# GpSimd's operations over 1024 and 768 elements, made in pieces of 256

## The chip, the cores and the metric

One core of a Trainium2 chip runs the whole program. The metric is the device time of one execution in microseconds; the median of three runs of the kernel before is 1775.95 us (1771.97 to 1776.2). Besides the runs there is one profiled execution, with a trace of every instruction.

Engines are called by their names: TensorE (PE in the rows; PEld is its weight load), VectorE (DVE), ScalarE (ACT), GpSimd (POOL) and SyncE (SP, which only issues DMAs here).

## The reference, cut to what matters

For each of 32 sequences of T = 512 tokens with C = 256 channels, in float32:

```python
x0 = x                                   # [32, 512, 256]
x = _layernorm(x)
# delta block
h = layernorm(x, dn_g, dn_b)
q, k, v = split(h @ gates_w + gates_b, 3); lr = h @ lr_w + lr_b
k = k / norm(k)
A = tril(k k^T, -1) + I
u = solve_triangular(A, v, lower=True)
y = (q k^T) @ (lr * u)
x = x + y @ out_w + out_b
# MLP
x = x + relu(layernorm(x, mn_g, mn_b) @ w1 + b1) @ w2 + b2
x = x0 + x
# gated FFN with int weights scaled by 1/127, hidden size 768
z = _layernorm(x)
out = x + (silu(z @ wg^T) * (z @ wu^T)) @ wd^T
```

## The kernel before, in words

A sequence is held as 128 partitions by TB = 4 blocks of C = 256 channels, so a whole sequence in SBUF is 1024 elements a partition. Products in full precision are made with split operands: a tile is rounded to its high part (names ending in `_hi`), the low part is the rest (`_lo`), and three matmuls are summed. Each low part is one subtraction of the high part from the whole.

There are two stages. The first one makes, for all sequences, the normalised keys (`kx`), the Gram matrices of the keys (`gg`, 4 diagonal blocks of 128 columns and, behind column OFF = 512, six blocks below the diagonal, 768 columns) and small inverses, and stores them in DRAM. The change does not touch it. The main stage is a loop over 34 rounds, pipelined by hand. In round i the attention part works on sequence i, the MLP and the gate and up products on sequence i-1, and the down product on sequence i-2. Round 0 has no MLP part, rounds 32 and 33 have no attention part.

The order on each engine is written out by hand, in one function per engine that is called once a round (`pe_body`, `dve_body`, `act_body`, `pool_body`); engines wait for each other by semaphores. Each engine takes its instructions in order, so a wait holds up all that stands behind it. What matters around the change, in the order of a round:

- VectorE makes `a0`, the sequence with the attention's result, and its statistics. GpSimd's `pool_norm` (lines 1437 to 1443, four instructions over 4 elements) turns them into scale and shift, and GpSimd and ScalarE normalise two blocks each into `xn` (lines 1450 and 1152).
- VectorE casts the 768 columns of `gg` to `gl_hi` (line 1321), and GpSimd makes `gl_lo` (line 1455).
- GpSimd adds `a0` to `xa`, giving `xa2` (line 1461; both read as xa in the rows), then makes the next `xa` from the input `xt` and the bias `b2_bc` (line 1466, read as 4 blocks with one bias row of 256). The second waits until the first is complete.
- GpSimd makes the normalised input `xh` in four instructions of 256 elements (line 1472). Behind the last one VectorE casts it to `xhm_hi` (line 1347), and GpSimd makes `xhm_lo` (line 1476).
- Between these VectorE makes `wt[3]` (line 1331), the high and low parts of the MLP's hidden layer, `h_hi(0)`, then `x128` (line 1218), `h_lo(0)`, `h_hi(1)`, `z_lo(3)`, `h_lo(1)` (lines 1281 and 1270), and behind the cast `xhm_hi` the combination `wt[2]` (line 1223).
- On TensorE `pe_zstep(3)` (line 938) needs `wt[3]` and `x128`; `pe_zstep(2)`, later in the round, needs `wt[2]`, which stands behind `xhm_hi` on VectorE. `pe_wstep(2)` needs `gl_lo`; `pe_bt(3)` needs `xhm_lo`; the transposes of `xh` (line 921) need `xhm_done`.
- GpSimd has another `pool_norm`, and then `hl`, four subtractions over 512 elements (line 1487).

SyncE reloads `gg` for the next round when `gl_lo` is done, and `xt` when `xb_done` (line 1467) is signalled.

Of the kernel before, what the change touches and what calls it, by code (L numbers as in the profile page):

```python
# [27 lines left out]
ALU = mybir.AluOpType  # L28
ACT = mybir.ActivationFunctionType
F32 = mybir.dt.float32  # L30
# [3 lines left out]
P = 128  # L34
# [7 lines left out]
def wait(eng, sem, value):  # L42

    if isinstance(value, int) and value <= 0:
        return
    eng.wait_ge(sem, value)


def delta_block_kernel(nc, x, dn_g, dn_b, gates_w, gates_b, lr_w, lr_b, out_w, out_b, mn_g, mn_b,
                       w1, b1, w2, b2, w_gate, w_up, w_down, out):  # L50
    NS, T, C = x.shape
    H = w_gate.shape[0]
    TB, CB, HB = T // P, C // P, H // P
    OFF = TB * P
    ROW = {3: OFF, 2: OFF + 3 * P, 1: OFF + 5 * P}
    GCOL = {(i, j): ROW[i] + j * P for i in ROW for j in range(i)}
    GW = OFF + 6 * P
# [25 lines left out]
    with ExitStack() as ctx:  # L83
        def sb(name, shape, dt=F32, c=ctx):
            return c.enter_context(nc.sbuf_tensor(name, shape, dt))
# [3 lines left out]
        def sem(name):  # L89
            held.append(nc.alloc_semaphore(name=name))  # L90
            return held[-1]
# [21 lines left out]
        def pair(name, shape, c=ctx):  # L113

            return sb(name + "_hi", shape, F32R, c=c), sb(name + "_lo", shape, F32R, c=c)
# [6 lines left out]
        b2_bc = sb("b2_bc", [P, C])  # L122
# [5 lines left out]
        xt = sb("xt", [P, TB, C])  # L128
        xh = sb("xh", [P, TB, C])
        xhT2 = pair("xhT", [P, CB, T])  # L130
        kx = sb("kx", [P, KXW])
        gg = sb("gg", [P, GW])
# [69 lines left out]
        with ExitStack() as pre:  # L202
# [293 lines left out]
            def pool_body(pool, i, par, first, left):  # L496
                if left == 2:
                    norms(pool, i + 2, par, 0)
                pool.wait_ge(sq_done, i + 1)
                wait(pool, kn_done, i)  # L500
                pool.tensor_tensor(rn[:, :], ssq[:, :], mhalf4[:, :], ALU.pow).then_inc(rn_done, 1)
                if left == 2:
                    norms(pool, i + 2, par, 1)
                prep_pool(pool, i - PREP)
                if i == INV_FIRST:
                    invert_start(pool, lanes0, 0)
                for q in range(INV_EACH * (i - INV_FIRST), INV_EACH * (i - INV_FIRST + 1)):
                    if 0 <= q < INV_STEPS:
                        invert_step(pool, lanes0, 0, q // 2, q % 2)
                    elif q == INV_STEPS:  # L510
                        invert_flip(pool, lanes0, 0, flipped0)

            def keys_pool(pool):
                for n in range(2):
                    norms(pool, n, n, 0)
                    norms(pool, n, n, 1)
                piped(pool_body, lambda e: None)(pool)
# [304 lines left out]
        with ExitStack() as mc:  # L822
            def mb(name, shape, dt=F32):
                return sb(name, shape, dt, c=mc)
# [6 lines left out]
            xhm2 = pair("xhm", [P, TB, C], c=mc)  # L831
            gl2 = pair("gl", [P, GW - OFF], c=mc)
# [5 lines left out]
            a0 = mb("a0", [P, TB, C])  # L838
# [6 lines left out]
            xa = mb("xa", [P, TB, C])  # L845
            xa2 = mb("xa2", [P, TB, C])
# [26 lines left out]
            xhm_hi, xhm_lo, gl_hi, gl_lo = sem("xhm_hi"), sem("xhm_lo"), sem("gl_hi"), sem("gl_lo")  # L873
# [4 lines left out]
            xb_done, xa_done, sh_done = sem("xb_done"), sem("xa_done"), sem("sh_done")  # L878
# [17 lines left out]
            def after(eng, sem, n, each=1):  # L896

                wait(eng, sem, min(n, NS) * each)
# [17 lines left out]
            with nc.Block() as block:  # L916
# [515 lines left out]
                def pool_norm(pool, n_done, read, n_read, mv_, ls, sc, steps, mvd, done):  # L1432

                    for k in range(CB):
                        after(pool, read[k], n_read)
                    pool.wait_ge(mvd, n_done)
                    pool.tensor_tensor(ls[:, 0, :], mv_[:, :, 1], eps4[:, :], ALU.add).then_inc(steps[0], 1)  # L1437
                    pool.tensor_tensor(ls[:, 1, :], zero4[:, :], mv_[:, :, 0], ALU.subtract).then_inc(steps[1], 1)
                    pool.wait_ge(steps[0], n_done)
                    pool.tensor_tensor(sc[:, 0, :], ls[:, 0, :], mhalf4[:, :], ALU.pow).then_inc(steps[2], 1)  # L1440
                    pool.wait_ge(steps[1], n_done)
                    pool.wait_ge(steps[2], n_done)
                    pool.tensor_tensor(sc[:, 1, :], sc[:, 0, :], ls[:, 1, :], ALU.mult).then_inc(done, 1)  # L1443

                def pool_body(pool, i, att, mlp, down, m, r):
                    if mlp:
                        pool_norm(pool, i, t3_ps, i - 1, mv2, ls2, sc2, l2, mv2_done, ln2_done)
                        pool.wait_ge(ln2_done, i)
                        for j in range(2):
                            op = pool.tensor_scalar(xn[:, j, :], a0[:, j, :], sc2[:, 0, j:j + 1], sc2[:, 1, j:j + 1],  # L1450
                                                    ALU.mult, ALU.add)
                        op.then_inc(xh2_done, 1)
                    if att:
                        pool.wait_ge(gl_hi, i + 1)
                        pool.tensor_tensor(gl2[1][:, :], gg[:, OFF:GW], gl2[0][:, :].bitcast(F32),  # L1455
                                           ALU.subtract).then_inc(gl_lo, 1)
                    if mlp:
                        for j in range(TB):
                            after(pool, x2_ev[j], i - 1)
                        pool.wait_ge(xb_done, i)  # L1460
                        pool.tensor_tensor(xa2[:, :, :], xa[:, :, :], a0[:, :, :], ALU.add).then_inc(xa_done, 1)  # L1461
                    if att:
                        wait(pool, xin, i * 16)
                        pool.wait_ge(kx_in, (i + 1) * 16)
                        after(pool, xa_done, i)
                        pool.tensor_tensor(xa[:, :, :], xt[:, :, :], b2_bc[:, :].unsqueeze(1).broadcast_to([P, TB, C]),  # L1466
                                           ALU.add).then_inc(xb_done, 1)
                        for k in range(CB):
                            after(pool, ht_ps[k], i)
                        after(pool, xhm_lo, i)  # L1470
                        for j in range(TB):
                            op = pool.tensor_scalar(xh[:, j, :], xt[:, j, :], kx[:, E_S + j:E_S + j + 1],  # L1472
                                                    kx[:, E_B + j:E_B + j + 1], ALU.mult, ALU.add)
                        op.then_inc(xhm_done, 1)
                        pool.wait_ge(xhm_hi, i + 1)
                        pool.tensor_tensor(xhm2[1][:, :, :], xh[:, :, :], xhm2[0][:, :, :].bitcast(F32),
                                           ALU.subtract).then_inc(xhm_lo, 1)
                    if mlp:
                        pool_norm(pool, i, t2_ps, i, mv3, ls3, sc3, l3, mv3_done, ln3_done)
                    if att:  # L1480
                        for j in range(TB):
                            after(pool, x2_ev[j], i)
                        pool.tensor_tensor(shf[:, :], kx[:, E_SH:E_SH + TB], zero4[:, :], ALU.add).then_inc(sh_done, 1)
                    for h in range(HB - 2):
                        if mlp:
                            pool.wait_ge(hh_ev[h], i)
                            pool.tensor_tensor(hl[:, h, :], hf[:, h % 2, :], hh[:, h, :].bitcast(F32),  # L1487
                                               ALU.subtract).then_inc(hl_ev[h], 1)

                @block.gpsimd  # L1490
                def _(pool):
                    overlapped(pool_body)(pool)
# [82 lines left out]
```

## Time and profile before

| | |
|---|---|
| median of 3 runs | 1775.95 us |
| profiled execution, its own time | 1777.43 us |
| span of its trace | 1775.1 us |
| mean granted TensorE clock | 0.983 |
| busy: TensorE matmul, VectorE, ScalarE, GpSimd | 1660.2, 1306.2, 774.0, 905.3 us |
| main stage, first and last GpSimd `gl_lo` start | 346.76 us, 1688.21 us |
| a steady round, from one `gl_lo` to the next | 43.30 us |

The profile has views that are used below: the chain of work that ended last, in order of time (what each step waited for, followed back from the end); groups of instructions by line with their mean duration; the instructions of an engine in order of time, with the idle time before each in brackets and what ended it; waits summed by who waited for whom; and stretches of time with the busy time and the granted TensorE clock. Matmuls are pipelined, so their durations overlap. Busy shares alone say little here, since the engines wait for each other within a round.

### The profile page before, as it was taken

What the parts mean: (1) busy time and instruction counts of PE and PEld (TensorE: products, weight loads), DVE (VectorE), ACT (ScalarE), POOL (GpSimd) and SP (SyncE); (2) the same over time, 40 slices, a digit from 0 to 9 for tenths busy, and PEclk for the clock granted to TensorE, in tenths of its full rate; (3) what the DMA queues carried; (4) which work ended last, traced back from release to release, by engine and by line L of the source; (5) the groups of instructions that cost most, each with busy time, mean ns of one, the idle gap of its engine ahead of it and who ended that gap; (6) DMA issues with size and microseconds to landing.
All of it is one profiled execution on the core that took longest, in us unless ns stands there. A gap on an engine that the chain in (4) does not pass through costs nothing.

```text
span 1775.1 us, 31629 instructions
## 1 busy us (share of the span) xinstructions
PE 1660.2 (94%) x11298; PEld 1505.6 (85%) x11298; DVE 1306.2 (74%) x2898; ACT 774.0 (44%) x1658; POOL 905.3 (51%) x1206
## 2 busy tenths in 40 slices
PE   5899999569999999999999999999999999999997
PEld 4899999468888888888888888888888888888886
DVE  4677777247888887788887777888877777777774
ACT  4677777114334333334344434344443333334442
POOL 4456776235555555555555555555555555555551
PEclk8999999789999999999999999999999999999999
DMA  4755565411111121111111211111112111121200
GB/s 114 240 185 192 193 212 191 167 43 43 54 55 55 55 90 54 55 55 55 63 57 55 90 54 55 55 54 55 55 54 78 55 55 55 56 63 61 62 13 24
DMA packets 131698, 145.32 MB, mean 82 GB/s; under 512 B 60885, under 2 KB 113368, under 8 KB 131544
## 3 DMA queue, kind: packets, MB, share of 16 engines
q1 hardware_dynamic: 131544, 143.31, 25.3%
q8 instruction: 91, 1.49, 0.4%
q14 instruction: 63, 0.52, 0.1%
HBM read 82.13 MB, written 61.15 MB: 81 GB/s over the span
## 4 chain that ended last, share of the span: by engine, by line
PE 45%; POOL 19%; issue 8%; DVE 7%; ACT 1%; POOLq 0%; DMA 0%; DVEq 0%; ACTq 0%
PE ps L153 22%; PE ps L1007 13%; POOL xh L1472 6%; POOL xa L1461 4%; POOL xa L1466 4%; PE ps L921 4%; PE ps L938 3%; PE ps L1017 3%; DVE bs L1418 2%; POOL xn L1450 2%; POOL sc L1440 2%; DVE a L1413 2%; DVE wt L1223 1%; POOL sc L1443 1%; PE ps L927 1%
## 5 line engine op out<-in xcount | busy, mean ns | idle before, releaser
L1487 POOL TENSOR_TENSOR hl<-hf,hh 128x512 fp32r<-128x512 f32 x128 | 167.1, 1305 | 406.2 <-ACT hh L1134 406.2
L1017 PE MATMUL ps<-wdT,hh 128*128 128x256 f32 x768 | 204.0, 303 | 0.8 <-ACT sg L1129 0.6
L1017 PE MATMUL ps<-wdT,hl 128*128 128x256 f32 x768 | 187.3, 281 | 2.0 <-DVE hl L1270 2.0
L1265 DVE TENSOR_TENSOR hf<-ps,sg 128x512 f32<-128x512 f32 x192 | 132.4, 690 | 66.2 <-PE ps L1007 63.6
L1134 ACT ACTIVATE hh<-hf 128x512 fp32r<-128x512 f32 x192 | 120.8, 629 | 135.0 <-DVE hf L1265 131.9
L1138 ACT ACTIVATE z_hi<-ps 128x256 fp32r<-128x256 f32 x128 | 49.4, 386 | 288.6 <-PE ps L938 288.6
L1129 ACT ACTIVATE sg<-ps 128x512 f32<-128x512 f32 x192 | 113.9, 593 | 126.4 <-PE ps L1007 126.4
L1007 PE MATMUL ps<-xh3T_hi,wgT 128*128 128x512 f32 x384 | 154.6, 403 | 1.1 <-DVE xh3T_lo L1270 1.1
L1007 PE MATMUL ps<-xh3T_hi,wuT 128*128 128x512 f32 x384 | 152.5, 397 | 0.0
L1007 PE MATMUL ps<-xh3T_lo,wgT 128*128 128x512 f32 x384 | 152.3, 397 | 0.0
L1007 PE MATMUL ps<-xh3T_lo,wuT 128*128 128x512 f32 x384 | 152.2, 396 | 0.0
L1017 PEld LDWEIGHTS ps<-wdT,hl 128*128 128x128 f32 x768 | 144.9, 189 | 4.0 <-DVE hl L1270 2.4
L1017 PEld LDWEIGHTS ps<-wdT,hh 128*128 128x128 f32 x768 | 144.9, 189 | 3.3 <-ACT sg L1129 1.3
L938 PE MATMUL ps<-wt,x 128*128 128x256 f32 x256 | 86.1, 418 | 40.0 <-issue 31.3
L1437 POOL TENSOR_TENSOR ls<-mv,eps 128x4 f32<-128x4 f32 x64 | 12.9, 202 | 196.7 <-DVE mv L1229 196.7
L1166 ACT ACTIVATE hf<-ps,b1f 128x512 f32<-128x512 f32 x64 | 44.1, 688 | 157.6 <-PE ps L153 157.6
L1472 POOL TENSOR_SCALAR xh<-xt,kx 128x256 f32<-128x256 f32 x128 | 111.6, 884 | 0.0
L927 PE MATMUL ps<-x,p 128*128 128x96 f32 (+2 forms) x768 | 102.8, 278 | 4.0 <-DVE p L1213 2.9
L927 PEld LDWEIGHTS ps<-x,p 128*128 128x128 f32 x768 | 99.3, 197 | 8.4 <-DVE p L1213 3.3
L1455 POOL TENSOR_TENSOR gl_lo<-gg,gl_hi 128x768 fp32r<-128x768 f32 x32 | 59.2, 1849 | 83.3 <-DVE gl_hi L1321 83.3
L1007 PEld LDWEIGHTS ps<-xh3T_hi,wgT 128*128 128x128 f32 x384 | 72.7, 189 | 27.1 <-ACT sg L1129 13.0
L1281 DVE CAST h_hi<-hf 128x512 fp32r<-128x512 f32 x64 | 82.2, 1284 | 18.0 <-ACT hf L1166 18.0
(218 smaller groups left out, 5678.5 us busy)
## 6 DMA issues: line engine op xcount, KB each, us to landing
gg_scratch<-gg SPq DMA_DIRECT2D x32, 640.0 KB, 3.4
gg<-gg_scratch SPq DMA_DIRECT2D x32, 640.0 KB, 3.9
kx_scratch<-kx SPq DMA_DIRECT2D x32, 522.0 KB, 2.9
kx<-kx_scratch SPq DMA_DIRECT2D x32, 522.0 KB, 3.7
xk<-in_L_attn_x_dram SPq DMA_DIRECT2D x32, 512.0 KB, 4.2
xt<-in_L_attn_x_dram SPq DMA_DIRECT2D x32, 512.0 KB, 4.8
out_dram<-ot SPq DMA_DIRECT2D x32, 512.0 KB, 2.9
low_scratch<-gg SPq DMA_DIRECT2D x128, 16.0 KB, 1.5
```

Of the source, the lines that this page charges most:

```text
L153: mm = pe.matmul(dst, a[ka], b[kb], start=start, stop=(stop and n == 0), **kw)
L921: mm = pe.transpose(ps[:, banks[k], blk(j)], src[:, j, blk(k)], ident[:, :])
L927: mm = pe.matmul(ps[:, bank, j * w:(j + 1) * w], lhs(j), rhs[:, j, c0:c0 + w], start=True, stop=True)
L938: pe.matmul(ps[:, A1, 0:C], x64[:, j, :], wt[:, j, :], start=True, stop=True).then_inc(z_ps[j], 1)
L1007: mm = pe.matmul(ps[:, bank, :], w[:, k, blk(h)], part[:, k, :], start=(k == 0 and part is x3h), stop=(k == CB - 1 and part is x3l))
L1017: mm = pe.matmul(ps[:, (FG, FU)[j // 2], (j % 2) * C:(j % 2 + 1) * C], part[:, h, blk(j)], wdT[:, h, :], start=(h == 0 and part is hh), st ...
L1129: act.activation(sg[:, h % 2, :], ps[:, FG, :], ACT.Silu, scale=QUANT).then_inc(sg_ev[h], 1)
L1134: act.activation(hh[:, h, :], hf[:, h % 2, :], ACT.Copy).then_inc(hh_ev[h], 1)
L1265: dve.tensor_tensor(hf[:, h % 2, :], ps[:, up_bank(h), :], sg[:, h % 2, :], ALU.mult).then_inc(hf_ev[h], 1)
L1281: dve.tensor_copy(h12[0][:, m, :], h1[:, m, :]).then_inc(h1_hi[m], 1)
L1472: op = pool.tensor_scalar(xh[:, j, :], xt[:, j, :], kx[:, E_S + j:E_S + j + 1], kx[:, E_B + j:E_B + j + 1], ALU.mult, ALU.add)
L1487: pool.tensor_tensor(hl[:, h, :], hf[:, h % 2, :], hh[:, h, :].bitcast(F32), ALU.subtract).then_inc(hl_ev[h], 1)
```

## The change

Four instructions of `pool_body` are written as loops over blocks of 256 elements. The semaphore is signalled by the last piece, and the waits stand ahead of the first one. The data and the order around them are the same, and the other engines' streams are unchanged.

```diff
-                        pool.tensor_tensor(gl2[1][:, :], gg[:, OFF:GW], gl2[0][:, :].bitcast(F32),
-                                           ALU.subtract).then_inc(gl_lo, 1)
+                        for c in range(0, GW - OFF, 2 * P):
+                            op = pool.tensor_tensor(gl2[1][:, c:c + 2 * P], gg[:, OFF + c:OFF + c + 2 * P],
+                                                    gl2[0][:, c:c + 2 * P].bitcast(F32), ALU.subtract)
+                        op.then_inc(gl_lo, 1)
...
-                        pool.tensor_tensor(xa2[:, :, :], xa[:, :, :], a0[:, :, :], ALU.add).then_inc(xa_done, 1)
+                        for j in range(TB):
+                            op = pool.tensor_tensor(xa2[:, j, :], xa[:, j, :], a0[:, j, :], ALU.add)
+                        op.then_inc(xa_done, 1)
...
-                        pool.tensor_tensor(xa[:, :, :], xt[:, :, :], b2_bc[:, :].unsqueeze(1).broadcast_to([P, TB, C]),
-                                           ALU.add).then_inc(xb_done, 1)
+                        for j in range(TB):
+                            op = pool.tensor_tensor(xa[:, j, :], xt[:, j, :], b2_bc[:, :], ALU.add)
+                        op.then_inc(xb_done, 1)
...
-                        pool.tensor_tensor(xhm2[1][:, :, :], xh[:, :, :], xhm2[0][:, :, :].bitcast(F32),
-                                           ALU.subtract).then_inc(xhm_lo, 1)
+                        for j in range(TB):
+                            op = pool.tensor_tensor(xhm2[1][:, j, :], xh[:, j, :], xhm2[0][:, j, :].bitcast(F32),
+                                                    ALU.subtract)
+                        op.then_inc(xhm_lo, 1)
```

GpSimd's stream in a round of the main stage, from its half of `xn` to the norm behind `xhm_lo`, in the kernel before:

```order
L1450 TENSOR_SCALAR xn<-a,sc 128x256 x2
L1455 TENSOR_TENSOR gl_lo<-gg,gl_hi 128x768
L1461 TENSOR_TENSOR xa<-xa,a 128x1024
L1466 TENSOR_TENSOR xa<-xt,b_bc 128x1024
L1472 TENSOR_SCALAR xh<-xt,kx 128x256 x4
L1476 TENSOR_TENSOR xhm_lo<-xh,xhm_hi 128x1024
L1437 TENSOR_TENSOR ls<-mv,eps 128x4
```

The same place in the changed kernel, whose lines from 1455 on are shifted:

```order
L1450 TENSOR_SCALAR xn<-a,sc 128x256 x2
L1456 TENSOR_TENSOR gl_lo<-gg,gl_hi 128x256 x3
L1464 TENSOR_TENSOR xa<-xa,a 128x256 x4
L1471 TENSOR_TENSOR xa<-xt,b_bc 128x256 x4
L1477 TENSOR_SCALAR xh<-xt,kx 128x256 x4
L1482 TENSOR_TENSOR xhm_lo<-xh,xhm_hi 128x256 x4
L1437 TENSOR_TENSOR ls<-mv,eps 128x4
```

Nothing changed its place; four instructions of a round became fifteen, eleven of them between `xn` and `xh` and four behind. On the other engines the streams are the same row for row.

## Rows read from the trace of the kernel before

**Rows 1.** Chain of waits, round 13: start us, us, what.
```profile
908.10 0.09 POOL gl_lo L1455
...
909.91 2.40 POOL xa L1461
...
914.85 3.55 POOL xh L1472 x4
...
918.42 0.07 DVE xhm_hi L1347
...
919.03 0.49 DVE wt L1223
```

**Rows 2.** Groups on GpSimd, 430 to 1700 us: busy us, mean ns | idle before.
```profile
L1487 POOL TENSOR_TENSOR hl<-hf,hh 128x512 fp32r<-128x512 f32 x116 | 151.6, 1307 | 368.7 <-ACT hh L1134 368.7
...
L1461 POOL TENSOR_TENSOR xa<-xa,a 128x1024 f32<-128x1024 f32 x30 | 71.6, 2387 | 0.0
...
L1455 POOL TENSOR_TENSOR gl_lo<-gg,gl_hi 128x768 fp32r<-128x768 f32 x30 | 55.5, 1851 | 54.2 <-DVE gl_hi L1321 54.2
```

**Rows 3.** VectorE in order of time, round 13: start us, us, instruction [idle before].
```profile
911.03 1.42 DVE L1331 TENSOR_SCALAR wt<-kx 128x256 f32<-128x256 f32 x1
912.85 2.28 DVE L1281 CAST h_hi<-hf 128x512 fp32r<-128x512 f32 x1 [0.41 <-ACT hf L1166]
915.05 0.28 DVE L1218 TENSOR_TENSOR x<-ps,x 128x128 f32<-128x128 f32 x1
915.25 0.84 DVE L1270 TENSOR_TENSOR h_lo<-hf,h_hi 128x512 fp32r<-128x512 f32 x1
916.02 0.41 DVE L1281 CAST h_hi<-hf 128x512 fp32r<-128x512 f32 x1
...
916.90 0.68 DVE L1270 TENSOR_TENSOR h_lo<-hf,h_hi 128x512 fp32r<-128x512 f32 x1
```

**Rows 4.** GpSimd: round 13; xh's duration min/median/max in ns; round 0.
```profile
903.34 0.20 POOL L1438 TENSOR_TENSOR ls<-zero,mv 128x4 f32<-128x4 f32 x1
903.49 1.01 POOL L1440 TENSOR_TENSOR sc<-ls,mhalf 128x4 f32<-128x4 f32 x1
...
912.46 2.39 POOL L1466 TENSOR_TENSOR xa<-xt,b_bc 128x1024 f32<-128x1024 f32 x1 [0.17 <-POOL xa L1461]
...
914.83 0.73 POOL L1472 TENSOR_SCALAR xh<-xt,kx 128x256 f32<-128x256 f32 x1
...
L1472 POOL TENSOR_SCALAR xh<-xt,kx x4: 559/906/1237, 914.8 to 917.8; 128x256 f32<-128x256 f32 x4
...
350.87 2.27 POOL L1472 TENSOR_SCALAR xh<-xt,kx 128x256 f32<-128x256 f32 x4
```

**Rows 5.** Waits of TensorE, 430 to 1700 us: us in total, times, longest.
```profile
PE ps L938 <- issue: 30.9, 30, 1.1
PE ps L938 <- DVE wt L1223: 8.1, 30, 0.3
PE ps L153 <- DVE bt_lo L1270: 0.9, 2, 0.5
```

**Rows 6.** xhm_lo on GpSimd, and TensorE's first product with xhm.
```profile
919.20 2.38 POOL L1476 TENSOR_TENSOR xhm_lo<-xh,xhm_hi 128x1024 fp32r<-128x1024 f32 x1 [0.81 <-DVE xhm_hi L1347]
...
923.02 0.36 PE L153 MATMUL ps<-z_hi,xhm_hi 128*128 128x256 f32 x1
```

**Rows 7.** Round 1: the four xh on GpSimd, and xhm_hi on VectorE.
```profile
393.51 2.79 POOL L1472 TENSOR_SCALAR xh<-xt,kx 128x256 f32<-128x256 f32 x4
...
397.74 0.68 DVE L1347 CAST xhm_hi<-xh 128x1024 fp32r<-128x1024 f32 x1
```

**Rows 8.** Stretches with busy us and PEclk (granted clock); transposes at either level.
```profile
375.70:377.90 2.20, 0.06 (x1) 0.00 (x0) 1.82 (x5) 0.63 (x1) 0.00 (x0) 1.00 0.00 0
...
1748.70:1755.30 6.60, 6.01 (x14) 4.79 (x15) 1.73 (x3) 2.90 (x5) 0.80 (x1) 0.50 0.21 78
...
386.95 1.96 PE L921 MATMUL ps<-ident,xn 128*128 128x128 f32 x8 [1.78 <-POOL xn L1450]
...
1747.12 1.09 PE L921 MATMUL ps<-ident,xn 128*128 128x128 f32 x8 [3.76 <-DVE xn L1248]
```

## What was predicted, before the changed kernel ran

> **What bounds the kernel now.** I read the chain of waits first, over one round of the main stage. From 908.10 us to 918.4 us it runs through GpSimd alone: gl_lo, xa (the add of a0), xa (the add of b2), four xh; then VectorE's cast xhm_hi, its wt and TensorE [rows 1]. The second view is GpSimd's durations by line: 1.85 us for 768 elements, 2.39 us for 1024, 1.31 us for 512 [rows 2]. The third is VectorE in the same stretch: a tensor_scalar of 256 elements that takes 1.42 us, a cast of 512 that takes 2.28 us, and the next such cast 0.41 us [rows 3]. The long ones end just behind the end of a GpSimd instruction: the cast at 912.85 + 2.28 = 915.13, with xa over at 912.46 + 2.39 = 914.85 [rows 3, 4]. So the two engines exclude each other for some of their operations. Fourth, TensorE's waits in rounds 2 to 31: 30.9 us in 30 times before a matmul of line 938, named "issue", which is pe_zstep(3), and 8.1 us in 30 times before pe_zstep(2), for wt; there is next to nothing else [rows 5]. That is 1.03 and 0.27 us a round. The first is x128's: its add starts at 915.05, behind the cast of 2.28 us, and ends at 915.33, and the step follows on it [rows 3]. The second is the end of the GpSimd chain.
>
> By the same view TensorE runs without a pause from pe_zstep(2) to the y products that release the next round, and VectorE, ScalarE and GpSimd's small norm lead on to gl_hi. So a round is as long as this loop, and what GpSimd takes between gl_lo and the last xh is in it in full. The 1.03 us before pe_zstep(3) is not: take it away and TensorE only waits longer before pe_zstep(2).
>
> **What the pieces cost by themselves.** From 512 to 1024 elements a tensor_tensor grows from 1.307 to 2.387 us: 2.109 ns an element, with 0.227 us left over, and 768 elements would be 1.847 us (1.851 measured) [rows 2]. A piece of 256 is then 0.767 us long. Instructions of 4 elements start 0.15 us apart though each is 0.20 long [rows 4], so 0.05 us lies under the one before. A piece takes about 0.71 us of the engine where a quarter of the long one takes 0.54: 0.17 us for each extra instruction. On the chain the change adds 2 (gl_lo) + 3 (xa) + 3 (xa) = 8 of them: 8 x 0.17 = 1.36 us, or by whole groups 3 x 0.71 + 0.05 - 1.85 = 0.33 and 2 x (4 x 0.71 + 0.05 - 2.385) = 1.01, together 1.34 us. I take 1.34. Bounds for one extra instruction: below, the slope with nothing fixed, 0; above, the whole left-over, 0.23.
>
> The three extra pieces of xhm_lo are off the chain: before, it starts at 919.20 and takes 2.38 us, and TensorE asks for it at 923.02, with pe_bt(3) [rows 6]; 0.5 us more still fits, and the order gives GpSimd nothing until the next norm. If the cover were gone it would be 0.5 us a round. The change moves no instruction on any other engine.
>
> **What the shared access gives back.** The four xh take 3.55 us in this round and 2.27 us in round 0, where VectorE has no MLP work [rows 1, 4]: 1.28 us is VectorE's doing. The pieces show whose: the first 0.73, the shortest 0.56, the longest 1.24 us, and from their median (0.906, the middle of 0.73 and the third) the third 1.08 [rows 4]. It is the end of h_hi(0), held back until 914.85, then h_lo(0) with h_hi(1) right behind it, and h_lo(1) [rows 3]. With the xa operations in pieces h_hi(0), which asks at 912.85, gets in at the first border, about when the first xa is over in its stretched form (913.2), where GpSimd pauses for 0.17 us anyway [rows 4]: nothing. h_lo(0) reads two tensors of SBUF and holds the access for some 0.52 us (the delay of the third xh piece, 1.08 - 0.56); at a border it runs beside the fixed part and the 0.05 us of overlap, so I take 0.30. h_hi(1) no longer follows on it, since it needs ScalarE's second relu: 0.25. h_lo(1): 0.30. wt, short, at a border: 0. Sum 0.85 in place of 1.28, a gain of 0.43. Bounds: all four fall into pauses (0) or all cost their undisturbed durations, 0.41 + 0.68 + 0.41 + 0.68 = 2.18 us [rows 3].
>
> So the chain grows by 1.34 - 0.43 = 0.9 us a round. Round 0 and round 1 pay nothing: in round 1 the last xh ends at 393.51 + 2.79 = 396.30 and VectorE casts it only at 397.74 [rows 7]. The last xa, in round 32, is alone on GpSimd, without a queue behind it. That leaves 30 rounds: 30 x 0.9 = 27 us. The profiled execution took 1777.4 us, with a span of 1775.1, so 1804; the median of the runs is 1775.95, 1.5 less, so 1803.
>
> On the sharing, the Trainium skill's page "SBUF — State Buffer" (SBUF: two separate sides) says that the pair of ports which VectorE and GpSimd share is an exclusive lock, taken for the whole instruction, for VectorE operations in a two-port mode or with two SBUF inputs. The trace agrees with who excludes whom (2.28 us for the cast), but not with the whole instruction: the third xh piece grew by 0.52 us beside an h_lo of 0.68. By the page the sum would be 1.34 - 1.28 + 2.18 = 2.24 us a round, the second rival's upper end.
>
> **Rivals.** *TensorE's clock falls.* x128 now comes before TensorE wants it, so TensorE is 1.03 us earlier and its pauses join before pe_zstep(2): 1.03 + 0.27 + 0.9 = 2.2 us. Of pauses this long the trace has both outcomes nearby: with 2.17 us at 375.8 the clock stayed at 2.4 GHz; after 3.76 us up to 1747.1 it was at 1.2 GHz from 1748.7 to 1755.3 [rows 8]. In such a stretch of 6.6 us TensorE takes nearly twice as long (1.96 us for eight transposes at 386.95, in such a stretch, against 1.09 at 1747.12) and sets the round: some 3.3 us lost. For it: 2.2 us is longer than any pause of the steady rounds. Against: just one pause a round, with dense work on both sides. If it strikes in 10 of 30 rounds, 33 us more: 1836; in all, 1902.
>
> *The access costs as much as before, or more.* VectorE gets in only behind a whole group of pieces, since GpSimd's next piece is queued and starts before the last has ended. Then the 1.28 us stays, the round grows by 1.34 us, and the time is 1776 + 40 = 1816; with all four operations paid in full it is 2.24 us and 1843. Against it: VectorE does get in between the xh pieces today, which are queued alike.
>
> *Not slower.* VectorE's operations drop into the fixed parts of the pieces and GpSimd gets its whole 1.28 us back, while an extra piece costs only the 0.15 us between the starts of two tiny ones: 8 x 0.15 - 1.28 = -0.08 us a round, 1774. It decides from the point where an extra piece costs no more than a border saves, 0.16 us. Against it: h_lo holds for 0.52 us, and no border is that long.
>
> *The pieces don't appear as such* (nothing on GpSimd's chain grows, because its stream of short instructions overlaps fully): 1776, hardly likely with 0.15 us between starts.
>
> **How the numbers follow.** Forecast 45%; clock 27%; access as dear as before 14%; not slower 11%; no effect 3%. What can be told from no change is 0.3%, 5.3 us. Slower by more: the first three, 0.86; the other two are shared about evenly, 0.07 and 0.07. The forecast's own range, with a round longer by 0.6 to 1.2 us, is 1794 to 1812. For 8 in 10 I go down to 1788 (0.4 us a round) and up to 1845, which takes in a clock that falls in 12 rounds and the dear access.
>
> **What would show it.** GpSimd's pieces at 0.76 us alone, starting 0.71 us apart; the time from gl_lo's first piece to the end of xh at 11.2 us instead of 10.3; the first h_hi near 0.6 us instead of 2.28; no pause before pe_zstep(3) and one of about 2.2 us before pe_zstep(2); rounds of 44.2 us instead of 43.3. I am wrong if the pieces start 0.6 us apart or less, if the last xh is not later, or if the granted clock is at 1.2 GHz in the rounds.

## The result, and the profile after

| | before | after |
|---|---|---|
| median | 1774.16 us (4 runs, 1771.97 to 1776.2) | 1807.9 us (4 runs, 1805.29 to 1811.15) |
| profiled execution, span | 1777.43, 1775.1 us | 1811.15, 1809.3 us |
| mean granted clock | 0.983 | 0.975 |
| a steady round, gl_lo to gl_lo | 43.30 us | 44.16 us, in six rounds some 1.56 us more |
| gl_lo of round 2 to gl_lo of round 31 | 1257.1 us | 1291.3 us |

The ratio is 1.0185, interval 1.016 to 1.0209: slower by about 33 us.

First the chain of waits in round 13 of the changed kernel, in order of time (start us, us, what); it answers to [rows 1].

```profile
921.07 0.09 POOL gl_lo L1456
921.16 0.61 issue
921.77 1.43 POOL gl_lo L1456 x2
923.20 2.81 POOL xa L1464 x4
...
929.61 2.60 POOL xh L1477 x4
932.21 0.02 issue
932.24 0.06 DVE xhm_hi L1347
```

It runs through the same GpSimd operations, now from 921.07 to 932.2: 11.14 us where it was 10.30 (908.10 to 918.40). The four xh are shorter (2.60 us, 3.55 in [rows 1]), everything ahead of them is longer.

VectorE in the same stretch answers to [rows 3].

```profile
924.00 0.73 DVE L1331 TENSOR_SCALAR wt<-kx 128x256 f32<-128x256 f32 x1
925.83 0.45 DVE L1281 CAST h_hi<-hf 128x512 fp32r<-128x512 f32 x1 [1.10 <-ACT hf L1166]
926.20 0.28 DVE L1218 TENSOR_TENSOR x<-ps,x 128x128 f32<-128x128 f32 x1
926.40 1.05 DVE L1270 TENSOR_TENSOR h_lo<-hf,h_hi 128x512 fp32r<-128x512 f32 x1
928.12 0.90 DVE L1281 CAST h_hi<-hf 128x512 fp32r<-128x512 f32 x1 [0.67 <-ACT hf L1166]
928.95 0.41 DVE L1270 TENSOR_TENSOR z_lo<-ps,z_hi 128x256 fp32r<-128x256 f32 x1
929.28 0.88 DVE L1270 TENSOR_TENSOR h_lo<-hf,h_hi 128x512 fp32r<-128x512 f32 x1
```

GpSimd's pieces of the second xa and of xh in this round (duration in ns, min/median/max, then first and last start) answer to xh's row in [rows 4]:

```profile
L1471 POOL TENSOR_TENSOR xa<-xt,b_bc x4: 733/820/1181, 926.2 to 928.7; 128x256 f32<-128x256 f32 x4
...
L1477 POOL TENSOR_SCALAR xh<-xt,kx x4: 554/557/989, 929.6 to 931.6; 128x256 f32<-128x256 f32 x4
```

One xa piece and one xh piece are far longer than the shortest. By the times it is VectorE's h_lo that had the access there: h_lo(0) and the xa piece of 1.18 us, which starts at 926.86, lie side by side, and so do h_lo(1) and the xh piece of 0.99 us, which starts at 929.60. The first h_hi takes 0.45 us in place of 2.28, wt 0.73 in place of 1.42: VectorE gets in at the borders of GpSimd's pieces. What it gained is not on the path, as TensorE's waits from 430 to 1730 us show (us in total, times, longest), beside [rows 5]:

```profile
PE ps L938 <- DVE wt L1223: 53.2, 29, 1.8
PE ps L153 <- DVE z_lo L1270: 6.1, 29, 0.2
PE ps L153 <- DVE bt_lo L1270: 0.9, 2, 0.4
```

The pause before `pe_zstep(3)` is gone, and the one before `pe_zstep(2)` went from 0.27 to 1.83 us. Last, the stretches right behind this pause in two rounds (busy us of PE, PEld, DVE, ACT, POOL, then the granted clock, DMA share and GB/s), beside [rows 8]:

```profile
444.80:448.10 3.30, 3.30 (x17) 3.30 (x17) 1.96 (x5) 0.18 (x1) 1.50 (x3) 0.50 0.00 0
1113.80:1117.10 3.30, 3.30 (x17) 3.30 (x17) 2.56 (x8) 0.13 (x1) 0.91 (x2) 0.50 0.00 0
```

TensorE is busy throughout, at 1.2 GHz. There are six such stretches in the main loop's steady rounds, none in the kernel before. The account of the 29 rounds between gl_lo of round 2 and gl_lo of round 31, in the profiled executions: 29 x 0.86 = 24.9 us, and 6 x 1.56 = 9.4 us, together 34.3 us, where 34.2 us were measured.

### The profile page after: what moved, and what is told of

It is laid out like the page before. It is cut to its first block, busy times and chain, and to the rows that moved or that the text cites. A ratio compares the mean times of both kernels' runs of the same rounds, so it can differ in the third digit from the quotient of the medians.

```text
span 1809.3 us, 31981 instructions
## 1 busy us (share of the span) xinstructions
PE 1675.1 (93%) x11298; PEld 1521.8 (84%) x11298; DVE 1259.2 (70%) x2898; ACT 770.8 (43%) x1658; POOL 947.7 (52%) x1558
## 4 chain that ended last, share of the span: by engine, by line
PE 44%; POOL 22%; issue 7%; DVE 6%; ACT 1%; POOLq 0%; DMA 0%; DVEq 0%; ACTq 0%
PE ps L153 21%; PE ps L1007 13%; POOL xa L1471 5%; POOL xa L1464 5%; POOL xh L1477 5%; PE ps L921 4%; PE ps L938 3%; PE ps L1017 3%; POOL gl_lo L1456 3%; DVE bs L1418 2%; POOL xn L1450 2%; POOL sc L1440 2%; DVE a L1413 2%; DVE wt L1223 1%; POOL sc L1443 1%
## 5 line engine op out<-in xcount | busy, mean ns | idle before, releaser
L1456 POOL TENSOR_TENSOR gl_lo<-gg,gl_hi 128x256 fp32r<-128x256 f32 x96 | 68.0, 738 | 83.2 <-DVE gl_hi L1321 83.2
L1471 POOL TENSOR_TENSOR xa<-xt,b_bc 128x256 f32<-128x256 f32 x128 | 108.8, 880 | 5.2 <-POOL xa L1464 5.2
L1482 POOL TENSOR_TENSOR xhm_lo<-xh,xhm_hi 128x256 fp32r<-128x256 f32 x128 | 89.9, 737 | 27.9 <-DVE xhm_hi L1347 27.9
L938 PEld LDWEIGHTS ps<-wt,x 128*128 128x128 f32 x256 | 42.1, 194 | 67.6 <-DVE wt L1223 62.2
```

Source lines behind the costliest of these rows:

```text
L938: pe.matmul(ps[:, A1, 0:C], x64[:, j, :], wt[:, j, :], start=True, stop=True).then_inc(z_ps[j], 1)
L1456: op = pool.tensor_tensor(gl2[1][:, c:c + 2 * P], gg[:, OFF + c:OFF + c + 2 * P], gl2[0][:, c:c + 2 * P].bitcast(F32), ALU.subtract)
L1471: op = pool.tensor_tensor(xa[:, j, :], xt[:, j, :], b2_bc[:, :], ALU.add)
```

## The experiments

All kernels are compared with the kernel before on the same chip; "round" is the time from one gl_lo to the next in the steady rounds of the profiled execution.

**One part at a time.** `e1_gl` is the kernel before with only gl_lo in pieces, `e2_xa` with only the two xa, `e3_lo` with only xhm_lo, each by the change's own edit. `e4_half` has the two xa in two pieces of 512:

```diff
-pool.tensor_tensor(xa2[:, :, :], xa[:, :, :], a0[:, :, :], ALU.add).then_inc(xa_done, 1)
+for j in range(0, TB, 2):
+    op = pool.tensor_tensor(xa2[:, j:j + 2, :], xa[:, j:j + 2, :], a0[:, j:j + 2, :], ALU.add)
+op.then_inc(xa_done, 1)
... the same for the add of b2
```

> Only gl_lo is made in pieces of 256, the rest as before. My theory (each extra instruction costs about 0.14 us of GpSimd, and what GpSimd takes from gl_lo to the last xh is in the round in full): three pieces take 2.09 us in the changed kernel's trace where the whole took 1.81, so the round grows by 0.28 us, 30 rounds by 8.4 us, 1782.6 us. Rival (the changed kernel is slower by the falls of TensorE's clock and by VectorE's waits, not by the pieces themselves): no difference here, 1774 us, since no VectorE operation contends in gl_lo's stretch and the pauses of TensorE hardly change.

Measured: 1784.5 us, ratio 1.0048 (1.0033 to 1.0063), round 43.56 us. The theory holds, and to its size: the round grew by 0.26 us, where 0.28 was expected.

> Only the two xa operations are made in pieces of 256. My theory: six extra instructions at 0.15 us are 0.90 us, of which the shared access gives back 0.28 (VectorE's claims cost GpSimd 1.09 us in place of 1.37): 0.62 us a round, and with a pause of some 1.55 us before pe_zstep(2) the clock stays whole: 1793 us. Rival (the access gives nothing back): 0.90 us a round, 1801 us, the first h_hi still short. Rival (the slowdown is gl_lo's or the clock's): below 1780 us.

Measured: 1806.58 us, ratio 1.0176 (1.0158 to 1.0195), round 44.10 us, eight rounds with a stretch at 1.2 GHz. The round grew by 0.80 us, between the theory (0.62) and its first rival (0.90), and I was wrong on the clock, which I had expected to stay whole. By itself this edit does nearly all of the change. GpSimd's rows of round 13 say why gl_lo's pieces add only 0.06 us on top:

```profile
921.98 2.84 POOL L1462 TENSOR_TENSOR xa<-xa,a 128x256 f32<-128x256 f32 x4
924.99 3.67 POOL L1469 TENSOR_TENSOR xa<-xt,b_bc 128x256 f32<-128x256 f32 x4 [0.17 <-POOL xa L1462]
928.65 2.60 POOL L1475 TENSOR_SCALAR xh<-xt,kx 128x256 f32<-128x256 f32 x4
```

Here h_hi(0) comes at 924.93, just as the second xa wants to begin (924.99), and that one's first piece takes 0.97 us where 0.73 is usual. In the changed kernel it comes into the pause between the two xa. What the shared access takes depends on such meetings.

> Only xhm_lo is made in pieces of 256. My theory: it takes 2.82 us in place of 2.38 and still ends at 922.0 by the times of the kernel before, 1 us ahead of pe_bt(3) at 923.02: rounds of 43.30 us, 1774 us. Rival (it is on the path behind another wait, or GpSimd's norm behind it comes late): 0.44 us a round, 1787 us.

Measured: 1777.19 us (10 runs), ratio 1.0003 (0.9987 to 1.002), round 43.30 us. No effect, as expected.

> The two xa operations are made in two pieces of 512, the rest is whole. My theory: two extra instructions cost 0.30 us a round, VectorE gets in at the borders nearly as well as with four pieces (h_hi(0) about 1.3 us long in place of 2.28), and the claims cost 0.2 to 0.3 us less than before: 0 to 0.1 us a round, 1774 to 1777 us. Rival (the access gives back only with a border at the very moment at which VectorE asks): 0.30 us a round, 1783 us. Rival (the borders are where VectorE's blocked operations pile up and cost more than before): above 1785 us.

Measured: 1783.64 us, ratio 1.0043 (1.0028 to 1.0058), round 43.63 us. The first rival was right: two extra instructions cost their 0.3 us, and the access gave nothing back. h_hi(0) still took 1.40 us, h_lo(0) 1.56.

**The price of a piece without VectorE's claims.** Both kernels, with VectorE's split of the hidden layer reduced:

```diff
-dve.tensor_copy(h12[0][:, m, :], h1[:, m, :]).then_inc(h1_hi[m], 1)
+dve.tensor_copy(h12[0][:, m, 0:8], h1[:, m, 0:8]).then_inc(h1_hi[m], 1)
... the same for h_lo, and both tiles zeroed once ahead of the loop
```

> The kernel before with h_hi and h_lo, VectorE's operations on the MLP's hidden layer, over 8 elements in place of 512 (the rest of the hidden layer's split is left out; the tiles are zeroed once). It takes VectorE's claims on the shared access away. My theory: the four xh take 2.2 to 2.3 us (3.55 before), the time from gl_lo to the end of xh falls from 10.28 to about 9.0 us, and a round is shorter by the 0.27 us that TensorE waits before pe_zstep(2) plus up to 1.0 us, as far as TensorE has no other limit: about 42.0 us. Rival (xh is slow by itself in the main stage, for its scalars or for another engine): the four xh stay at 3.5 us.

> The changed kernel with the same left out as in the run before. My theory: from gl_lo to the end of xh 2.09 + 2.80 + 0.21 + 2.80 + 2.2, about 10.1 us, 1.15 to 1.2 us more than the kernel before without claims; so the pieces alone cost 8 x 0.147 us, and the 0.86 us of the full kernels is this less what the access gives back. Rival (pieces cost by their contention with VectorE only): both kernels take the same time from gl_lo to the end of xh.

Measured, one execution each: 1747.68 and 1768.76 us, rounds of 42.50 and 43.07 us. GpSimd in round 13, whole operations, then pieces:

```profile
894.80 1.85 POOL L1459 TENSOR_TENSOR gl_lo<-gg,gl_hi 128x768 fp32r<-128x768 f32 x1 [1.81 <-DVE gl_hi L1321]
896.61 2.38 POOL L1465 TENSOR_TENSOR xa<-xa,a 128x1024 f32<-128x1024 f32 x1
899.16 2.38 POOL L1470 TENSOR_TENSOR xa<-xt,b_bc 128x1024 f32<-128x1024 f32 x1 [0.17 <-POOL xa L1465]
901.52 2.16 POOL L1476 TENSOR_SCALAR xh<-xt,kx 128x256 f32<-128x256 f32 x4
```

```profile
906.71 2.13 POOL L1460 TENSOR_TENSOR gl_lo<-gg,gl_hi 128x256 fp32r<-128x256 f32 x3 [1.81 <-DVE gl_hi L1321]
908.78 2.84 POOL L1468 TENSOR_TENSOR xa<-xa,a 128x256 f32<-128x256 f32 x4
911.80 2.81 POOL L1475 TENSOR_TENSOR xa<-xt,b_bc 128x256 f32<-128x256 f32 x4 [0.17 <-POOL xa L1468]
914.59 2.16 POOL L1481 TENSOR_SCALAR xh<-xt,kx 128x256 f32<-128x256 f32 x4
```

The four xh fall to 2.16 us in both: the slow xh was VectorE's doing. From gl_lo's start to the end of xh it is 8.88 and 10.04 us, so eight extra instructions cost 1.16 us, 0.145 each, with next to no contention for GpSimd: its longest piece in this stretch is 0.77 us. VectorE's wt and, in `e5_before_noclaim`, its reduced cast still had to wait. Even a cast of eight elements took 1.99 us there, until the whole xa was over (899.16 + 2.38 = 901.54):

```profile
899.58 1.99 DVE L1281 CAST h_hi<-hf 128x8 fp32r<-128x8 f32 x1 [0.43 <-ACT hf L1166]
```

The rounds differ by less (0.57 us), since without pieces another wait, 0.75 us before `pe_zstep(3)`, sets the round.

**The clock.** The changed kernel, with TensorE kept at work in its pause:

```diff
+for q in range(6):
+    pe.matmul(ps[:, A1, 0:C], w22[0][:, 0, blk(0)], w22[0][:, 0, :], start=True, stop=True)
 pe_zstep(pe, i, 2)
```

> The changed kernel with six matmuls of 256 columns ahead of pe_zstep(2), into the bank that it overwrites; they run in the pause. My theory (the clock falls where the pause of 1.83 us meets it badly, and each fall costs 1.56 us): the pause is 1.1 us, no stretch at 1.2 GHz in the rounds, all rounds at 44.16 us (and the two with the flip of the inverse at 44.85), some 8 us less than the profiled execution of the changed kernel, about 1801 us, and less spread between runs. Rival (the falls come from something else, or the long rounds are DMA or VectorE): again rounds of 45.7 us, 1807 us.

Measured: 1797.77 us (1796.82 to 1798.93), ratio 1.0121 (1.0106 to 1.0137). All steady rounds take 44.13 us but two, which take 44.87 (the same two are 0.7 us longer in the kernel before); there is no stretch at 1.2 GHz in them, and the pause is 1.12 us. That is 10 us less than the changed kernel's median for 192 matmuls more. So the falls come from the pause: filled in part, it let the clock fall in none of these rounds. Between the two profiled executions gl_lo of round 2 to gl_lo of round 31 is shorter by 9.9 us (1291.3 against 1281.4), the size of six falls. The four runs say the same: their mean granted clocks are 0.983 to 0.985, the changed kernel's 0.975 to 0.979. Of what the two spans differ by beyond that (14.5 us in all), 3.5 us lie ahead of round 2, so not all of the gain is the pause's.

**A better order.** Since xa's second operation is wanted only a round later, the same work can stand elsewhere. First `e8_xh_first`: the four xh ahead of both xa, whole; `e9b_xh_first_pieces` is the same with the xa in pieces.

```diff
 pool.tensor_tensor(gl2[1]...)              # gl_lo
+for j in range(TB): op = pool.tensor_scalar(xh[:, j, :], ...)   # moved up with its waits
 pool.tensor_tensor(xa2...)                 # xa
 pool.tensor_tensor(xa...)
-for j in range(TB): op = pool.tensor_scalar(xh[:, j, :], ...)
```

> The kernel before with xh made ahead of the two xa operations, nothing in pieces. My theory (the chain from gl_lo to xh sets the round): the chain is 2.2 to 2.6 us in place of 8.5 behind gl_lo, xhm_hi no longer waits for it, the 0.27 us before pe_zstep(2) goes, and TensorE's 1.03 us before pe_zstep(3) becomes the limit that is left, since h_hi(0) now stands behind xa (VectorE asks at 912.85, xa would run from 912.3 to 914.7): between 42.2 and 43.0 us a round, 1740 to 1765 us. Rival (the GpSimd chain only seems to be the bound, the round is set by the total of TensorE's work and pauses elsewhere): 43.3 us and 1774 us.

Measured: 1793.45 us, ratio 1.0102 (1.0082 to 1.0121), rounds of 43.81 and 43.95 us. My theory failed, and so did the rival: it is slower than before. VectorE's rows:

```profile
915.17 1.89 DVE L1281 CAST h_hi<-hf 128x512 fp32r<-128x512 f32 x1 [1.16 <-ACT hf L1166]
916.98 0.28 DVE L1218 TENSOR_TENSOR x<-ps,x 128x128 f32<-128x128 f32 x1
917.18 2.69 DVE L1270 TENSOR_TENSOR h_lo<-hf,h_hi 128x512 fp32r<-128x512 f32 x1
```

The cast waits for the first xa, h_lo for the whole second one; z_lo(3) stands behind them, and TensorE waits 1.15 us for it.

> xh ahead of the two xa operations as in the run before (which was slower: VectorE's h_hi(0) took 1.89 us and its h_lo(0) 2.69 us behind whole xa operations, so z_lo(3) came late and TensorE waited 0.65 and 1.14 us), now with the xa operations in pieces of 256. My theory (whole operations cost VectorE, pieces cost GpSimd; here GpSimd's chain ends early and VectorE is the one in need): h_hi(0) and h_lo(0) about 0.5 to 1.1 us, TensorE's waits below 0.4 us together, rounds of 42.0 to 42.5 us: 1737 to 1755 us, and the pieces win against the same order without them. Rival (pieces cost in any order): rounds of 44.5 us or more.

Measured: 1768.5 us (10 runs, 1756.06 to 1775.41), ratio 0.9961 (0.9939 to 0.9984). In this order pieces win 25 us over whole operations, as the theory said, but the time missed the expected 1737 to 1755 us. The rounds are of two kinds, 42.33 us and 43.8 us; the profiled execution, with nine of the second kind, is the fastest of the ten. The first rows below are VectorE's h_hi(0) and GpSimd's xa (two of its four pieces) in a long round, the last one h_hi(0) in a short round:

```profile
905.67 2.43 DVE L1281 CAST h_hi<-hf 128x512 fp32r<-128x512 f32 x1 [1.49 <-ACT hf L1166]
...
905.03 1.41 POOL L1472 TENSOR_TENSOR xa<-xa,a 128x256 f32<-128x256 f32 x2
...
949.49 0.92 DVE L1281 CAST h_hi<-hf 128x512 fp32r<-128x512 f32 x1 [1.17 <-ACT hf L1166]
```

In the short rounds the cast asks 0.08 to 0.09 us after a piece has started and gets in behind it. In the long ones it asks 0.04 to 0.08 us before a piece starts, and then stays out for three more pieces, until the group of four is over.

Then `e10b_xb_late`, the second xa behind GpSimd's norm, whole, with nothing in pieces, and `e11b_xb_late_pieces`, the changed kernel with the same move:

```diff
-after(pool, xa_done, i)
-pool.tensor_tensor(xa[:, :, :], xt...)     # between xa2 and xh
...
 pool.tensor_tensor(shf...)                 # the last step of the norm
+after(pool, xa_done, i)
+pool.tensor_tensor(xa[:, :, :], xt...)
```

> The kernel before with its second xa operation (the add of b2) moved behind GpSimd's norm, where GpSimd waits 8 us for hh; nothing in pieces. My theory: 2.55 us leave the chain from gl_lo to xh, which ends about 1.9 us before VectorE asks for it; h_hi(0) waits for one xh piece at most, so both pauses of TensorE (1.03 and 0.27 us) go: rounds of 42.0 us, 1737 us (up to 42.4 us, 1748 us, if z_lo(3) is a little late). Rival (the access puts VectorE's operations and xh in each other's way all the same): rounds above 42.8 us, 1760 us.

> The changed kernel (all pieces) with its second xa operation moved behind the norm in the same way. My theory (pieces cost time only on a bound chain): the chain has about 1.9 us of slack and the pieces of gl_lo and the first xa need 0.74 of it, so the same rounds as without pieces, within 0.1 us: within 3 us of the run with whole operations. Rival (a piece costs its 0.15 us wherever it stands): 15 pieces for 4, at least 0.7 us a round, 21 us more.

Measured: 1777.55 us, ratio 1.0009 (0.9996 to 1.0022), round 43.22 us, for the whole operation, and 1747.05 us, ratio 0.9834 (0.9807 to 0.9861), round 42.43 us, with pieces. Both expectations failed, and it was the same step: I had not asked which other VectorE operations want the access at the new place. VectorE's first two xn instructions (line 1248), whole operation, then pieces:

```profile
922.60 2.95 DVE L1248 TENSOR_SCALAR xn<-x,sc 128x256 f32<-128x256 f32 x2
```

```profile
914.35 1.73 DVE L1248 TENSOR_SCALAR xn<-x,sc 128x256 f32<-128x256 f32 x2
```

In both the chain up to xh had its slack, and the two old pauses of TensorE were gone. But a new one of 1.58 us stood behind xn in the first, and two of some 0.38 us each in the second. The whole xa kept the first xn out for 2.62 us, the pieces for less. So pieces do help, by 30 us here, where GpSimd has time and VectorE is on the path.

Last, `e12b_xb_after_xn`, the same move, whole, but not before xn is made:

```diff
 pool.tensor_tensor(shf...)
+if mlp:
+    pool.wait_ge(xh3_done, i)
 after(pool, xa_done, i)
 pool.tensor_tensor(xa[:, :, :], xt...)
```

> The kernel before with the second xa operation moved behind the norm as in the run that gained nothing, and, new, not started before VectorE has made xn (line 1248; a wait on xh3_done); nothing in pieces. In the run without this wait the whole xa stood over VectorE's first xn instruction (2.62 us in place of 0.40) and TensorE waited 1.58 us for it, all its pauses of the round. My theory (a whole GpSimd operation costs when VectorE asks for the access on the path, and nothing otherwise): xn 0.4 us each, xa at a place where VectorE works from PSUM, TensorE without a pause: rounds of 43.22 - 1.58 = 41.65 us, 1726 us, faster than the changed kernel with the same move (1747 us). Rival (the next VectorE operation with two SBUF inputs, the inverse's subtraction or m_lo, is on the path as well): rounds of 42.2 us or more, 1743 us or more.

Measured: 1719.84 us (5 runs), ratio 0.9685 (0.9666 to 0.9703), round 41.50 us: faster than both kernels, by 57 us against the kernel before (1777.25 us beside it), and close to the theory's 41.65 us and 1726 us. The waits of TensorE from 430 to 1650 us are one row; the rows behind it are GpSimd's last step of the norm and the moved operation, and VectorE beside it, which works from PSUM (ps) and takes its usual times:

```profile
PE ps L153 <- DVE bt_lo L1270: 0.9, 2, 0.5
```

```profile
900.45 0.20 POOL L1480 TENSOR_TENSOR shf<-kx,zero 128x4 f32<-128x4 f32 x1
902.85 2.40 POOL L1484 TENSOR_TENSOR xa<-xt,b_bc 128x1024 f32<-128x1024 f32 x1 [2.19 <-DVE xn L1248]
...
902.69 0.68 DVE L1296 SCALAR_TENSOR_TENSOR ot<-ps,x2k 128x512 f32<-128x512 f32 x1
903.33 0.42 DVE L1270 TENSOR_TENSOR z_lo<-ps,z_hi 128x256 fp32r<-128x256 f32 x1
904.15 1.29 DVE L1270 TENSOR_TENSOR xh3T_lo<-ps,xh3T_hi 128x512 fp32r<-128x512 f32 x2 [0.39 <-ACT xh3T_hi L1144]
```

## Why the prediction was right

The forecast was 1803 us, slower, and the measured 1807.9 us lies in its range. The main mechanism, extra instructions on GpSimd's chain at a price that the shared access gives back only in part, is what the runs show. That the number came so close is partly luck: two terms were off by amounts that nearly cancel, and the falling clock, which was a rival and not the forecast, did a part of the slowing. By the sign that the prediction itself names (a granted clock at 1.2 GHz in the rounds) it was wrong on this part. Step by step:

- *The bound.* It was as read. GpSimd's time from gl_lo to the last xh is in the round in full: it grew by 0.84 us (10.30 to 11.14), and the round by 0.86 us (43.30 to 44.16). `e3_lo` shows the other side: pieces off this chain cost nothing that can be told from noise (ratio 1.0003).
- *The price of a piece.* The mechanism was right, the size too high. A piece is 0.74 us long and they start 0.70 us apart (gl_lo's three span 2.13 us, xa's four 2.84), so an extra instruction costs 0.145 us (e5 against e6) and not 0.17: 1.16 us a round in place of 1.34. The 0.15 us between the starts of two tiny instructions [rows 4] was the better guide, and I had used it only for a rival. (The 0.54 us for a quarter of the long operation is its slope alone; a quarter of 2.39 us is 0.60. The sum by whole groups doesn't use it.)
- *What the shared access gives back.* Too high as well. It was to be 0.43 us, and it is 1.16 - 0.86 = 0.30. h_hi(0) did fall into the pause between the two xa, at no cost. But both sides of this term were too low. Undisturbed, the four xh take 2.16 us (e5), not the 2.27 of round 0, so VectorE's claims were 1.4 us before the change and not 1.28. Behind it they are 1.1 us and not 0.85: one piece of the second xa took 1.18 us where 0.735 is free, 0.44 us for h_lo(0) and not 0.30; another took 0.91, 0.17 us for h_hi(1) and not 0.25; and the first xh took 0.99 in place of 0.56, 0.43 us for h_lo(1) and not 0.30. The errors of the price and of what is given back nearly cancel, 0.18 against 0.13. `e2_xa` and `e4_half` show that this term is the least certain of all: with other borders it gave back 0.1 us and nothing.
- *The two pauses of TensorE.* The first is gone, as forecast. The second is 1.83 us and not 2.2, because 0.21 us went to a new short wait for z_lo(3), which stands behind the blocked h_hi(1). The chain's growth of 0.86 and not 0.9 takes 0.04 more. The rest, 0.12 us, is open.
- *The clock.* I gave the falling clock 27% and 3.3 us for each fall. It did fall, in 6 of 30 rounds of the profiled execution, for 3.4 us a time, at a loss of 1.56 us: 9.4 of its 34 us. So the rest of the forecast was some 2 us too high, and with this term the whole came out low, by 5 us on the median; without the falls the time would be between the 1797.8 us of `e7_fill` and the profiled 1811.15 - 9.4 = 1801.8 us. My stretch of 6.6 us came from the end of the program [rows 8], where the pauses around it were longer. The trace of the kernel before spoke more strongly for this rival than I allowed. In round 1 the clock was at 1.2 GHz too, and the last two pauses ahead of it were 2.13 us and 1.78 us [rows 8, the transposes at 386.95], no longer than the 2.17 us behind which it had stayed:

```profile
384.04 1.13 PE L927 MATMUL ps<-x,p 128*128 128x96 f32 x8 [2.13 <-DVE p L1213]
...
386.80:393.40 6.60, 6.45 (x25) 5.88 (x25) 2.07 (x4) 1.59 (x5) 6.43 (x4) 0.50 0.33 103
```

Why it falls in some rounds and not in others, behind the same pause of 1.83 us, is open.

- *The other rivals.* That VectorE gets in only behind a whole group did not happen in this kernel (the longest h_hi of its steady rounds is 0.93 us), though `e9b_xh_first_pieces` shows that it can. "Not slower" came to -0.08 us a round, 0.94 less than measured: it had the price of a piece right, but the access gave back 0.30 us and not all of its 1.28.

On the lock that the Trainium skill's page "SBUF — State Buffer" (SBUF: two separate sides) describes, the traces bear out the exclusion: in `e8_xh_first` a cast and an h_lo of 0.41 and 0.68 us undisturbed took 1.89 and 2.69 us behind whole xa. The time for which GpSimd is held back is again less than the whole VectorE instruction: 0.44 us in the changed kernel, by an h_lo that takes 0.68 us undisturbed.

## What to carry to other kernels

In these runs, cutting an operation on GpSimd costs 0.15 us for each extra instruction and mostly lets VectorE in at the borders; it pays where VectorE is the one waited for (25 and 30 us here) and costs where GpSimd's chain sets the round (33 us here, with the clock's part). Better than either is to place the long operation where the other engine doesn't ask for SBUF: look in the trace, at the place it would move to, for the kinds of VectorE operation that were kept out here (casts and tensor_scalar from SBUF to SBUF, and subtractions with both inputs in SBUF), and for what stands behind them. And when pauses of TensorE join to one, look at the granted clock behind it, also in the first and last rounds of the trace at hand.

## What the runs showed of the hardware

- The cast's place in time decides how long it is kept out: asked for 0.08 to 0.09 us after a GpSimd piece has started, it took 0.92 to 0.94 us; asked for 0.04 to 0.08 us before, it took 2.43 to 2.48 us, with three borders passed by. Nine of the thirty steady rounds of `e9b_xh_first_pieces` were of the second kind in its profiled execution, and its ten runs spread from 1756 to 1775 us. Why a border is passed by is open.
- A pause of 1.83 us a round let the granted clock fall to 1.2 GHz in six and in eight rounds of 30 (the changed kernel and `e2_xa`), one of 1.2 us (`e4_half`) in none; one of 1.58 us (`e10b_xb_late`), at another place in the round, in none either. Each count is from one profiled execution.
- VectorE's tensor_scalar with two scalars (xn, 0.40 us by itself) is kept out by GpSimd just as its casts are: 2.62 us behind a whole xa (`e10b_xb_late`).
- How little VectorE has to do doesn't shorten its wait: the cast of eight elements took 1.99 us behind a whole xa (`e5_before_noclaim`).
